# Second layer of a two-layer perceiver: the three engines' stage order, with stages of three tiles interleaved on TensorE

## What is computed

```python
x = x + _L0_xattn_ref(_layernorm(x, axis=-1), ...)
x = x + _L0_attn_ref(_layernorm(x, axis=-1), Wq, bq, Wk, bk, Wv, bv, Wo, bo)
x = x + _L0_ffn_ref(_layernorm(x, axis=-1), ...)
...
```

## Time and profile before

| | us |
|---|---|
| runs | 2096.43, 2103.98, 2104.85 |
| median | 2103.98 |
| profiled execution, its own time | 2095.2 |
| its span, first to last instruction | 2092.7 |
| PE busy over the span | 1685.8 (81%) |
| DVE busy | 1584.6 (76%) |
| ACT busy | 1194.4 (57%) |
| POOL busy | 602.0 (29%) |

### The profile page before, as it was taken

One profiled execution on the slowest core, in us unless ns is written; L12 is line 12 of the kernel. 1 busy time (PEld: TensorE's weight loads), 2 busy tenths in 40 slices (PEclk: granted clock), 3 DMA queues, 4 the chain that ended last, 5 costly groups with the idle time before them and its releaser, 6 DMA issues.

```text
span 2092.7 us, 45479 instructions
## 1 busy us (share of the span) xinstructions
PE 1685.8 (81%) x13802; PEld 1233.6 (59%) x13802; DVE 1584.6 (76%) x4308; ACT 1194.4 (57%) x3322; POOL 602.0 (29%) x734
## 2 busy tenths in 40 slices
PE   6999999999999877756658989898989787863373
PEld 4677777777777655523336666666667566642241
DVE  6688888888888745779947888888887278874395
ACT  2466565665655534445535666666667467652493
POOL 0122222222222200001114444444443145434342
PEclk9999999999999989988978999999999789975797
DMA  2011111111111150030002222222211100000124
GB/s 96 18 29 28 29 29 32 28 28 29 29 33 28 37 127 1 1 108 1 1 19 73 62 61 61 61 61 61 52 35 33 28 13 12 12 12 18 51 78 150
DMA packets 119515, 87.10 MB, mean 42 GB/s; under 512 B 76991, under 2 KB 95746, under 8 KB 118660
## 3 DMA queue, kind: packets, MB, share of 16 engines
q1 hardware_dynamic: 116484, 79.71, 14.4%
q0 software_dynamic: 2944, 6.37, 0.9%
HBM read 72.05 MB, written 12.21 MB: 40 GB/s over the span
## 4 chain that ended last, share of the span: by engine, by line
PE 36%; DVE 30%; issue 16%; ACT 12%; POOL 2%; DVEq 1%; DMA 1%; ACTq 1%; SPq 1%; POOLq 0%
PE ps L669 3%; PE ps L1929 3%; PE ps L691 3%; PE ps L1857 3%; ACT a_pr L403 2%; DVE a_pT L532 2%; DVE a_nm L524 2%; PE ps L737 2%; DVE d_ks L1726 2%; PE ps L1006 2%; PE ps L1908 2%; PE ps L1867 2%; PE ps L707 1%; ACT d_pr L1660 1%; POOL f_row_store L2520 1%
## 5 line engine op out<-in xcount | busy, mean ns | idle before, releaser
L403 ACT ACTIVATE a_pr<-ps,a_nm 128x257 f32<-128x257 f32 x512 | 238.2, 473 | 174.3 <-DVE a_nm L524 174.3
L532 DVE COPY a_pT<-ps 128x512 f32<-128x512 f32 x256 | 170.3, 686 | 60.0 <-PE ps L707 59.5
L1680 ACT ACTIVATE d_pr<-d_st,d_nm 128x257 f32<-128x257 f32 x256 | 128.1, 502 | 128.4 <-DVE d_nm L1789 127.1
L330 POOL TENSOR_TENSOR a_sf<-a_sf,a_ratio 128x256 f32<-128x256 f32 x64 | 39.5, 617 | 474.1 <-DVE a_ratio L553 474.1
L524 DVE TENSOR_REDUCE a_nm<-ps 128x2 f32<-128x514 f32 x256 | 174.5, 682 | 0.0
L707 PE MATMUL ps<-ident,a_pr 128*128 128x128 f32 x1024 | 159.0, 278 | 0.0
L1908 PE MATMUL ps<-d_kc,d_qc 128*128 128x257 f32 x512 | 142.1, 400 | 14.7 <-DVE d_vc L1765 14.7
L1588 POOL TENSOR_TENSOR d_kc<-d_kc,d_ks 128x257 f32<-128x257 f32 x64 | 60.2, 941 | 265.9 <-ACT d_dist L1645 130.6
L707 PEld LDWEIGHTS ps<-ident,a_pr 128*128 128x128 f32 x1024 | 120.6, 143 | 25.6 <-issue 12.7
L669 PE MATMUL ps<-a_cT,a_wqk 128*128 128x257 f32 x512 | 132.7, 381 | 1.9 <-ACT a_v L393 0.8
L678 PE MATMUL ps<-a_wvg,a_cT 128*128 128x256 f32 x512 | 127.6, 392 | 0.0
(11 more groups left out here) (385 smaller groups left out, 4385.4 us busy)
## 6 DMA issues: line engine op xcount, KB each, us to landing
a_cT<-in_ctx SPq DMA_DIRECT2D x64, 257.0 KB, 2.6
d_cT<-in_ctx SPq DMA_DIRECT2D x64, 257.0 KB, 2.8
f_wf<-in_f_w SPq DMA_DIRECT2D x24, 512.0 KB, 3.7
a_vbd<-a_vself SPq DMA_DIRECT2D x256, 8.0 KB, 1.8
d_lp<-d_pr SPq DMA_DIRECT2D x256, 0.5 KB
e_vb<-e_vs SPq DMA_DIRECT2D x256, 8.5 KB, 1.8
f_yab<-f_y_store SPq DMA_DIRECT2D x16, 256.0 KB, 5.9
c_wf<-in_c_w SPq DMA_DIRECT2D x3, 1024.0 KB, 7.3
```

What stands on the lines that cost most here:

```text
L403: ins = act.activation(pr[j][:, g, :], ps[:, S_BANK[u % 2] + k, S:LK], ACT.Exp, bias=nm[j][:, g:g + 1], accum_out=ssum[j][:, 0, g:g + 1])
L532: dve.tensor_copy(pT[u][:, :, :, :], ps[:, T_BANK[u % 2], :].rearrange("p (g c q) -> p g c q", g=2, c=2))\
L1680: ins = act.activation(pr[j][:, g, :], st[u][:, k, :], ACT.Exp, bias=nm[u][:, k:k + 1], accum_out=sm[j][:, g:g + 1])
```

## The change

`front` and `back` are taken apart on PE, ACT and DVE, and the pieces are put in another order. No instruction is added or removed; `b_v` gets a second buffer, and the wait of `values_out` on W moves two tiles back.

On PE a row of before is the turn from one tile to the next: T, Q, V and S of tile t+1, then TW, W and P of tile t (in the names, `ps` is the accumulator memory, `ident` marks a transpose).

The diff, cut to its core:

```diff
-        v = sb("b_v", [P, HID])
+        v = [sb(f"b_v{j}", [P, HID]) for j in range(2)]
...
             def values_out(t):
                 act.wait_ge(v_psum.sem, v_psum.at(t, 1))
-                act.wait_ge(o_psum.sem, o_psum.at(t, 0))
-                act.activation(v[:, :], ps[:, 2, 0:HID], ACT.Copy).then_inc(v_ready.sem, 1)
+                if t >= 2:
+                    act.wait_ge(o_psum.sem, o_psum.at(t - 2, 1))
+                act.activation(v[t % 2][:, :], ps[:, 2, 0:HID], ACT.Copy).then_inc(v_ready.sem, 1)
...
-            def back(t, more=True):
+            def exps(t):
                 act.wait_ge(sub_done.sem, sub_done.at(t, 1))
                 act.activation(sc[:, :, :], sc[:, :, :], ACT.Exp).then_inc(exp_done.sem, 1)
-                if 0 <= t - ABS_AT < 6:
-                    absolute((t - ABS_AT) // 2, (t - ABS_AT) % 2)
-                if more:
-                    front(t + 1)
+
+            def step(t):
                 act.wait_ge(pT_psum.sem, pT_psum.at(t, 1))
                 act.activation(pT[:, :, :], ...)
+                if t + 1 < NT:
+                    exps(t + 1)
                 act.wait_ge(o_psum.sem, o_psum.at(t, 1))
                 act.activation(oT[:, :, :], ...)
-                if more:
-                    values_out(t + 1)
+                if t + 2 < NT:
+                    queries_out(t + 2)
+                    values_out(t + 2)
+                if t + 3 < NT:
+                    input_out(t + 3)
+                if 0 <= t - ABS_AT < 6:
+                    absolute((t - ABS_AT) // 2, (t - ABS_AT) % 2)
...
+            input_out(0)
+            queries_out(0)
             values_out(0)
-            for t in range(NT - 1):
-                back(t)
-            back(NT - 1, False)
+            input_out(1)
+            exps(0)
+            queries_out(1)
+            values_out(1)
+            input_out(2)
+            for t in range(NT):
+                step(t)
...
                 if 0 <= t - TERNARY_AT < 6:
                     ternary((t - TERNARY_AT) // 2, (t - TERNARY_AT) % 2)
+                if t + 2 < NT:
+                    front(t + 2)
                 dve.wait_ge(exp_done.sem, exp_done.at(t, 1))
...
-            front(0)
+            turn(0)
+            queries(0)
+            values(0)
+            turn(1)
             for k in range(KT):
                 pe.matmul(ps[:, 7, 0:HID], lhsT=bvT[:, k, :], rhs=wo[:, k, :], start=(k == 0), stop=False)
...
-            for t in range(NT - 1):
-                front(t + 1)
-                back(t)
-            back(NT - 1)
+            scores(0)
+            queries(1)
+            values(1)
+            turn(2)
+            scores(1)
+            for t in range(NT):
+                turn_weights(t)
+                if t + 2 < NT:
+                    queries(t + 2)
+                weigh(t)
+                if t + 2 < NT:
+                    values(t + 2)
+                project(t)
+                if t + 3 < NT:
+                    turn(t + 3)
+                if t + 2 < NT:
+                    scores(t + 2)
```

More of the change, by code:

```diff
@@ L870, in scalar, with input_out @@
             norm_scalar(act, n)
-            def front(t):
+            def input_out(t):
                 act.wait_ge(xT_psum.sem, xT_psum.at(t, 1))
@@ L876, in front, with queries_out @@
                     .then_inc(xT_ready.sem, 1)
+            def queries_out(t):
                 act.wait_ge(qk_psum.sem, qk_psum.at(t, 1))
@@ L985, in vector @@
             softmax(0, True)
-            for t in range(1, NT - 1):
-                front(t + 1)
+            for t in range(1, NT):
                 softmax(t)
                 add(t - 1)
-            softmax(NT - 1)
-            add(NT - 2)
             add(NT - 1)
@@ L995, in tensor, with turn @@
             pe.wait_ge(w_loaded.sem, w_loaded.at(1, 0))
-            def front(t):
+            def turn(t):
                 pe.wait_ge(xn_ready.sem, xn_ready.at(t, 1))
@@ L1001, in front, with queries @@
                 ins.then_inc(xT_psum.sem, 1)
+            def queries(t):
                 pe.wait_ge(xT_ready.sem, xT_ready.at(t, 1))
@@ L1009, in front, with values @@
                 ins.then_inc(qk_psum.sem, 1)
+            def values(t):
                 pe.wait_ge(v_ready.sem, v_ready.at(t, 0))
@@ L1014, in front, with scores @@
                 ins.then_inc(v_psum.sem, 1)
+            def scores(t):
                 pe.wait_ge(qk_ready.sem, qk_ready.at(t, 4))
@@ L1021, in front, with turn_weights @@
                 ins.then_inc(s_psum.sem, 1)
-            def back(t):
+            def turn_weights(t):
                 pe.wait_ge(p_ready.sem, p_ready.at(t, 1))
@@ L1027, in back, with weigh @@
                 ins.then_inc(pT_psum.sem, 1)
+            def weigh(t):
                 pe.wait_ge(pT_ready.sem, pT_ready.at(t, 1))
@@ L1031, in back, with project @@
                     m, r = h // 2, slice(64 * (h % 2), 64 * (h % 2) + 64)
-                    ins = pe.matmul(ps[r, 6, m * P:m * P + P], lhsT=v[:, h * DH:h * DH + DH], rhs=pT[:, h, :],
+                    ins = pe.matmul(ps[r, 6, m * P:m * P + P], lhsT=v[t % 2][:, h * DH:h * DH + DH], rhs=pT[:, h, :],
                                     start=True, stop=True)
                 ins.then_inc(o_psum.sem, 1)
+            def project(t):
                 pe.wait_ge(o_ready.sem, o_ready.at(t, 1))
```

## The result

The changed kernel takes 2063.61 us, median of four runs (2061.80 to 2064.75), beside 2100.95 for the kernel before (four runs, taken with them): a ratio of 0.982, interval [0.980, 0.984], 37 us less. The forecast was 2067. A second set gave 2060.56 (2056.14 to 2064.51) beside 2097.73, ratio 0.983 [0.980, 0.987]. The profiled execution of the first set took 2064.5 with a span of 2061.7; that of the second, of the same kernel, 2056.14 with 2053.7.

What follows compares the result with a forecast made beforehand. A chain of PE and ACT taking turns bounds the phase; 30.3 us saved between first and last TW, with the start 34, gave 2061 on the profiled execution, 2070 on the median; 2067 was taken, range 2053 to 2080.

Steps and rivals of the forecast that it cites:

- The chain: Ordinary turns: PE and ACT hand-overs set the old 8.24 us; covered by other stages, the turn is 5.8 us.
- the sums: PE's sums ahead of P, at most 0.73 us each time: two covered in `ternary` turns, one costs some 0.5.
- PE and ACT arriving together: End of an ordinary turn: both engines reach the next TW at 5.8 us, 0.5 above the softmax's own 5.27.
- Extra work: Turns with additional instructions: `absolute` costs nothing, `ternary` turns take 6.9 us, `scale` groups cost 0.9 in all.
- The start: Before the first TW: Q of tile 1 runs beside the first exponential, a gain of 3.6 us.
- The tail: Behind the last TW, 900.26 to 904.80 before the change: the same instructions, so no gain or loss counted.
- Rival D: PE at 1.2 GHz for the whole phase: turns about 10 us, 22 us slower, 2117 or 2126; chance 0.03.
- The sum: First to last TW 94.5 us instead of 124.75, saving 30.3; with the start 34; phase ends at 871.
- A: Extra work adds up: `ternary` turns 7.8 us, ordinary ones towards 6.2; gain 25 to 29; chance 0.20.
- B: Softmax binds everywhere: ordinary turns 5.3 us, `ternary` ones 6.75; gain 39; chance 0.13.
- C: POOL's bias addition meets DVE's multiplication: six turns lose 0.19 to 0.73 us each; gain 30 to 33; chance 0.05.
- E: One hand-over stays on the chain: turns average 7.9 us or more, gain under 10; chance 0.04.

## Why the prediction was right

**The chain, and what takes its place.** Right. The hand-overs of the earlier trace rows are covered as they were walked, and PE's order binds: the sums on PE lengthen a turn by 0.44, 0.99 us more of DVE lengthen one by 0.45 only, and with the copy of W out of the exponential's way it is 0.06 shorter. The turn was forecast at 5.8 and is 5.81. Terms in it are off and cancel nearly: from T to S it is 0.53 instead of 0.36 (0.17 of it is "issue"), from the exponential to the copy of W 0.53 instead of 0.63, so that P starts 3.89 behind TW and not 3.99; V's loads end at 3.69 instead of 3.43, so that P waits 0.20 and not 0.56. "PE and ACT arriving together" was close.

**Extra work.** `absolute` at nothing: right. `ternary` 6.9: it is 6.79, nearer the lower figure of 6.75. A `scale` in such a turn costs 0.40 (7.19 - 6.79), forecast 0.45; the sums once 0.44, forecast 0.5; the turn without T 5.59, forecast 5.8. Together 93.54 against 94.5.

**The start** gained 4.5 instead of 3.6: the first TW comes 13.7 us behind the first norm, 18.2 before. From the exponential on it is as walked. The term that was mis-sized is the exponential itself, which I left where it was: it starts 11.30 behind the first norm (767.77 - 756.47) instead of 12.09. The products for `b_yb` now stand ahead of the first scores on PE and not behind them, so DVE's copy of `b_yb`, which the first softmax stands behind, comes 1.12 sooner; the scores, now the later of the two, leave 0.79 of it. Q of tile 1, 2.05 instead of 3.08, is not on this chain.

**The tail is the term that was mis-sized most**: 4.54 forecast, 6.78 in the first profile. I walked the ordinary turn and concluded that PE's longest idle would be 1.1 us. In the last two turns there is no Q and no V to fill: PE idles 0.93 before W and 2.12 before P, whose copy stands behind the exponential. That this alone doesn't settle the clock, the second execution shows, with the same idle and 4.55 us. Rival D named the right mechanism and was right that it would not decide; it cost 2.2 us at one place, in some executions.

**The sum.** Turns 31.2 (forecast 30.3), start 4.5 (3.6), tail -2.2 (0): 33.5 against 34, with errors that cancel; that the sum agrees to half a microsecond is luck. In the second execution it is 31.2, 5.2 and 0, together 36.4: there the tail is as forecast, and the first TW comes 13.04 behind the first norm (770.24 - 757.20). The phase ended at 870.45, forecast 871; 0.85 of what it ended earlier is that it began so much earlier in this execution. The span fell by 31.0, and in the second execution by 39.0; the difference lies mainly behind the phase and in the tail. The median fell by 37, and came out 3 us below 2067; the phase gives 33.5 of it in the first execution and 36.4 in the second. Single executions of the kernel before lie up to 15 us apart, of the changed one up to 9, and what of the 3 us is that stays open.

**The rivals.** A: T does wait for the norm behind the pair, but within DVE's turn, so nothing adds up. B: no, PE binds at 5.81, not DVE at 5.3. C didn't happen, by 0.03 us: POOL ends at 817.25, the multiplication starts at 817.28. What it would have cost the multiplication was not measured; another step of DVE lost 0.39 us with 0.58 of the 0.73 us addition beside it, within my bounds of 0.19 to 0.73 and less than the wait for the whole that the prediction named. E: no.

## What to carry to other kernels

When no engine is full, follow one turn through the list and look for the brackets that name the other engine; put a stage of another tile into each, and check that the instruction which feeds the earliest stage (here the norm, worth 1.6 us a turn) isn't queued behind the latest. Then walk the first and the last turns separately, where the filling work is missing: there waits come back, and with them perhaps a lower clock. When you move work to another engine beside a busy one, look at the form of the instruction as well as its length.

## What the runs showed of the hardware

- A POOL addition of two tensors slowed a DVE instruction with two tensors in SBUF (the memory that holds the `b_` and `c_` buffers) beside it: 1.68 us instead of 0.69 with additions beside it throughout, 1.67 instead of 1.28 with 0.58 us of one. It is less than a full wait: 0.58 of the addition was left when the 1.28 us step began, and it lost 0.39. POOL can lose too: the bias addition behind the long one took 1.18 instead of 0.73, while the one beside the 1.67 us step kept its 0.73. A DVE addition with one operand in the accumulator memory kept its 0.41.
- A POOL comparison of one tensor with a constant, 2.77 to 2.87 us for 128x1024, slowed nothing that was seen beside it: multiplication, subtraction, sum and maximum took 0.67 to 0.69.
- The granted clock can fall to 0.50 behind a stretch in which PE has 0.99 us of work in 3.50, and it can stay at 1.00 behind the same instructions, 1.05 in 3.50. With the copy of W first it fell behind 2.17 us of work in 3.50 and none in the next 1.50; the kernel before has the same two figures ahead of its last TW and kept 1.00. What decides between them no run here shows.
